# A two-level product whose next block's waits stand among the last terms of the current one

## The reference

```
gi = x_t @ W_ih + b_ih          # 64 x 1536
gh = h @ W_hh + b_hh            # 64 x 1536
r, z = sigmoid(i_r + h_r), sigmoid(i_z + h_z)
n = tanh(i_n + r * h_n)
h = (1 - z) * n + z * h
...
x + down( silu(gate(h)) * up(h) )   # operands quantised to fp8
```

## Time and profile before

| what | value |
|---|---|
| median of three runs | 2875.44 us (2875.31 to 2877.52) |
| profiled execution | its span is 2879.2 us; no other time is recorded for it |
| TensorE busy with matmuls | 2562.9 us, 89% of the span |
| DVE, ACT, POOL busy | 59%, 40%, 44% |
| matmuls at L1145 (whole) | 32768, mean 324 ns, 1026.0 us busy |
| matmuls at L1153 (low) | 16384, mean 324 ns, 756.5 us busy |
| mean granted clock of TensorE | 0.959 |

### The profile page before, as it was taken

The page is one execution under the profiler, slowest core; times in us unless marked ns, Lnnn a source line. Parts: engine busy times, 40 slices in busy tenths (PEclk is TensorE's granted clock), DMA queues, the critical chain, the costliest instruction groups (busy, mean ns, idle before and its releaser), DMA issues. The chain is left out here.

```text
span 2879.2 us, 154632 instructions
## 1 busy us (share of the span) xinstructions
PE 2562.9 (89%) x67605; PEld 1681.0 (58%) x67605; DVE 1685.2 (59%) x3398; ACT 1140.6 (40%) x2317; POOL 1262.3 (44%) x598
## 2 busy tenths in 40 slices
PE   2088999998889999999999999999996999999995
PEld 1066777776768888887675564655642444444442
DVE  8852222225632222225646778867592888888887
ACT  1321222225632222224702333323232777777773
POOL 0255666662046666664061363622700333333334
PEclk8599999999999999999999999999998999999998
DMA  6833222224422222226554253442432223232322
GB/s 193 239 85 77 74 73 71 73 71 112 131 63 71 74 73 70 73 71 167 152 135 127 92 151 118 115 156 85 129 143 93 74 84 95 84 95 84 95 63 53
DMA packets 234843, 293.74 MB, mean 102 GB/s; under 512 B 69581, under 2 KB 194023, under 8 KB 233895
## 3 DMA queue, kind: packets, MB, share of 16 engines
q1 hardware_dynamic: 212743, 240.84, 30.6%
q10 hardware_dynamic: 18304, 36.19, 3.6%
q0 software_dynamic: 3680, 15.21, 1.9%
HBM read 231.61 MB, written 60.45 MB: 101 GB/s over the span
## 5 line engine op out<-in xcount | busy, mean ns | idle before, releaser
L1145 PE MATMUL psum<-second_shared 64*32 64x384 f16 x32768 | 1026.0, 324 | 50.2 <-issue 31.3
L1153 PE MATMUL psum<-low_w,low_hot 64*32 64x384 f16 x16384 | 756.5, 324 | 2.0 <-issue 2.0
L1372 DVE TENSOR_SCALAR second_shared<-psum 32x384 f16<-32x384 f32 x496 | 272.3, 549 | 749.1 <-PE psum L1145 741.9
L953 POOL TENSOR_TENSOR low_hot<-first_shared,sum_mask 128x1024 f16<-128x1024 f16 x256 | 499.8, 1952 | 430.1 <-DVE first_shared L1359 183.8
L1145 PEld LDWEIGHTS psum<-second_shared 64*32 64x32 f16 x32768 | 561.5, 93 | 198.0 <-issue 89.8
L947 POOL TENSOR_TENSOR second_shared<-first_shared,whole_mask 128x2048 f16<-128x2048 f16 x128 | 462.5, 3614 | 460.1 <-PE psum L1145 348.2
L1044 ACT ACTIVATE second_shared<-psum 32x384 f16<-32x384 f32 x496 | 239.8, 483 | 801.9 <-PE psum L1145 795.9
L1233 PE MATMUL psum<-low_w,low_hot 64*64 64x384 f16 x12288 | 513.7, 326 | 19.9 <-issue 13.5
L1233 PEld LDWEIGHTS psum<-low_w,low_hot 64*64 64x64 f16 x12288 | 378.3, 108 | 150.4 <-issue 18.4
L310 PE MATMUL psum<-w_x,x_cols 128*64 128x512 f32 (+1 forms) x1856 | 312.0, 495 | 9.5 <-ACT x_cols L280 9.5
L1153 PEld LDWEIGHTS psum<-low_w,low_hot 64*32 64x32 f16 x16384 | 282.5, 93 | 56.8 <-issue 3.1
(11 more groups left out here) (286 smaller groups left out, 2746.6 us busy)
## 6 DMA issues: line engine op xcount, KB each, us to landing
low_w<-w_rows SPq DMA_DIRECT2D x384, 144.0 KB
low_w<-w_rows SPq DMA_DIRECT2D x256, 120.0 KB
second_shared<-w_rows SPq DMA_DIRECT2D x1024, 24.0 KB, 1.9
x_gates<-x_out ACTq DMA_DIRECT2D x58, 384.0 KB, 2.3
xg<-x_gates SPq DMA_DIRECT2D x58, 384.0 KB, 3.2
low_w<-w_rows SPq DMA_DIRECT2D x256, 72.0 KB
low_w<-w_rows SPq DMA_DIRECT2D x384, 48.0 KB
w_rows<-quantised SPq DMA_DIRECT2D x24, 384.0 KB, 4.9
```

Of the source, the lines that this page charges most:

```text
L953: nc.gpsimd.tensor_tensor(low_hot[:, buf].rearrange("p (s k) b -> p s k b", s=SUBS), low_a[:, slot, bass.ds(c, 1), :, :].rearrange("p a s ...
L1145: last = nc.tensor.matmul(run[m][u][j * Q:(j + 1) * Q, :], whole_hot[rows[u], m, sign, kk, j % 2 * Q:(j % 2 + 1) * Q], whole_w[rows[u], m, ...
L1153: nc.tensor.matmul(run[m][u][j * Q:(j + 1) * Q, :], low_hot[rows[u], m, kk, j % 2 * Q:(j % 2 + 1) * Q], low_w[rows[u], m, at:at + UC], sta ...
L1372: last = nc.vector.tensor_scalar(whole_w[u * B:u * B + Q, m, 0, bq, :], run[m][u][bq * Q:(bq + 1) * Q, :], 1.0 / HIGH_ONE, None, ALU.mult)
```

## The change

The block's waits become four functions, each with its own register work. They are called for the *next* block behind terms 11, 12, 13 and 14 (counted from 0) of the current one: low loads, whole loads, bases, hot rows. Before the loop they are made once for block (0, 0). The loop runs over c = 0 to 30; the turn c = 31 is written out behind it, its second block with no waits. For a turn with a constant c no register work is made. Each function waits for a constant first and then for the register's value, so there are eleven waits a block where nine were.

```
-                            with pe.Fori(0, NBK) as c:
+                            def bases_ready(c, m):
+                                based = c * 2 + (fine_no(t, m, 0) + 1)
+                                if not isinstance(c, int):
+                                    pe.compute_val(based)
+                                pe.wait_ge(base_v[0], fine_no(t, m, 0) + 1)
+                                for u in range(2):
+                                    pe.wait_ge(base_v[u], based)
+                                    pe.wait_ge(base_a[u], based)
+
+                            def weights_ready(c, m):
+                                w_ready = c * LOADED + (loaded_before(stage_of(t, m), m) + LOADED)
+                                if not isinstance(c, int):
+                                    pe.compute_val(w_ready)
+                                pe.wait_ge(w_in[m], loaded_before(stage_of(t, m), m) + LOADED)
+                                pe.wait_ge(w_in[m], w_ready)
...
+                            def terms(c, m, following):
+                                for kk in range(BK):
+                                    term(m, kk)
+                                    if following:
+                                        then = (c, 1) if m == 0 else (c + 1, 0)
+                                        if kk == BK - 5:
+                                            weights_ready(*then)
+                                        elif kk == BK - 4:
+                                            whole_ready(*then)
+                                        elif kk == BK - 3:
+                                            bases_ready(*then)
+                                        elif kk == BK - 2:
+                                            hots_ready(*then)
+
+                            weights_ready(0, 0)
+                            whole_ready(0, 0)
+                            bases_ready(0, 0)
+                            hots_ready(0, 0)
+                            with pe.Fori(0, NBK - 1) as c:
                                 for m in range(2):
-                                    based = c * 2 + (fine_no(t, m, 0) + 1)
...
-                                    for kk in range(BK):
-                                        term(m, kk)
+                                    terms(c, m, True)
+                            terms(NBK - 1, 0, True)
+                            terms(NBK - 1, 1, False)
```

More of the change, by code:

```diff
@@ L1165, in term @@
                                         last.then_inc(run_ok[u], 1)
-                            with pe.Fori(0, NBK) as c:
-                                for m in range(2):
-                                    based = c * 2 + (fine_no(t, m, 0) + 1)
[L1170 to L1181, removed]
-                                    for kk in range(BK):
-                                        term(m, kk)
@@ new lines, in weights_ready, with whole_ready @@
+                            def weights_ready(c, m):
[4 more added lines that the diff above has]
+                                pe.wait_ge(w_in[m], w_ready)
+                            def whole_ready(c, m):
+                                ready = c * WHOLE_LOADED + (t * NBK + 1) * WHOLE_LOADED
+                                if not isinstance(c, int):
+                                    pe.compute_val(ready)
+                                pe.wait_ge(whole_in[m], (t * NBK + 1) * WHOLE_LOADED)
+                                pe.wait_ge(whole_in[m], ready)
@@ new lines, in hots_ready @@
+                            def hots_ready(c, m):
+                                ready = c * 2 + (block_no(t, m, 0) + 2)
+                                if not isinstance(c, int):
+                                    pe.compute_val(ready)
+                                pe.wait_ge(hot_ok, block_no(t, m, 0) + 2)
+                                pe.wait_ge(hot_ok, ready)
+                            def terms(c, m, following):
[11 more added lines that the diff above has]
+                                            hots_ready(*then)
```

## The result

The changed kernel takes 2993.28 us, the median of four runs (2986.77 to 2998.96), against 2876.03 us: ratio 1.0407, 95% interval 1.0391 to 1.0422. That is +117 us where +99 was forecast; 2993 lies inside the range of 2960 to 2998. Here the profiled execution's own time is given too: 2998.96 us for a span of 2997.2, so 1.8 us lie around a span.

The account below looks back on a forecast made before the run. TensorE's time plus its holes was taken to bound the kernel. The terms 88 + 4.5 + 1.5 + 5 = +99 us, added to the 2875.44 us median, gave about 2975 us, range 2960 to 2998.

Parts of the forecast that it names:

- (b), the ring: Whole-load wait behind a block's 13th term closes a ring: period 8.96 us against 8.18, +0.78 a block, 88 us.
- (a), the hidden waits: Waits leave the border between blocks: gain 0.11 us inside a turn, 0.45 of 0.65 us at a return.
- (c), low loads, bases, hot rows: Their moved waits: low loads 0 to 0.1 us late, bases and hot rows there before the restart; nothing added.
- The bases' group: Five waits right behind the restart: 0 to 0.1 us a block, taken as 0, 11 us kept for the range.
- rival 3: The waits' own cost shows as well: +11 to +22 us, 2986 to 2997 us; chance 12%.
- (d), the written-out turns: Last turn of each product, new code to fetch: 0 to 4 us, taken as 2.5 each, +5 us.
- the first blocks: First product's first ten blocks: about 4.5 us, plus 1.5 us for a late load awaited three terms sooner.
- Rival 1: Loads are not late, so only the gain from hidden waits counts: 30 us faster, 2845 us; chance 4%.
- Rival 2: Granted clock falls to half for the three terms behind the hold: +165 us, 3140 us; chance 3%.
- Rival 4: Longer loop no longer stays on chip, each turn paying 3 us: +100 to +180, 3075 to 3155 us; chance 2%.

Follow-up runs that it names:

- fewer_loads_shifted: The changed kernel with a block's eight whole loads issued as four of twice the size, second product's loop shifted half a page: 2846.45 us, ratio 0.9889.
- last_turn_out: The kernel before, waits still at the head of each block, with only the last turn of each product written out: 2890.91 us, ratio 1.0043.
- late_whole: The changed kernel with the wait for the whole loads alone put back to the border, behind term 15: 3115.67 us, ratio 1.0825.
- changed_fewer_loads: The changed kernel with a block's eight whole loads issued as four of twice the size, loop not shifted: 3062.03 us, ratio 1.0606.
- by_arrival: The changed kernel with its waits ordered bases, hot rows, low loads, whole loads: 2950.01 us, spread 2910.37 to 3028.79, no ratio given.

## Why the prediction was right, point by point

- **(b), the ring.** Right in mechanism and nearly in size: 9.02 us a block where 8.96 was forecast, +0.85 where +0.78. 111 blocks (51 and 60) came to +94 us against 88 for 113. Three positions of the wait bear it out: four, three and one term behind it gave 9.51, 9.02 and 8.03 us, and loads in time gave 7.85.
- **(a), the hidden waits.** Under-sized, without consequence: I kept 0.2 us at a return, it became 0.02. Whatever a wait, the register work and the branch need is covered by the sequencer's lead once the awaited thing is there.
- **(c), low loads, bases, hot rows.** "Covered by (b) in any case" held for the sum. But the hold is a real one: between 887 and 1387 us the low loads are named for 15.1 us beside 25.0 for the whole ones, and without the whole loads' hold theirs makes 8.36 us a block. The bases' group (five waits here, six of the nine in the kernel before) costs nothing, and rival 3 (own cost) falls with the 7.85 us of fewer_loads_shifted.
- **(d), the written-out turns: the term that was mis-sized.** The forecast had 5 us, from the "issue" waits at L1145 alone in the first turn. Measured alone it is 14.1 us, and 15.7 in the changed kernel. Holes at L1153 belong to it too, so that a turn costs 5.7 us in the first product where I had 3 before hiding; in the second one hole alone is 3.1 us long (last_turn_out), and in the changed kernel the load for block 63 came 4.4 us later than before, with 3.4 us of waiting. 15.7 us lies outside the 0 to 8 that I had allowed this term. The total stayed inside the range because the 11 us kept for the bases' group were not needed; that is luck. This term is most of what was missing; the first blocks (+9.4 against 6) and the ring (+6) are the rest.
- **Rival 1** (faster) needed the landings before 6.0 us. fewer_loads_shifted made them so, and then it came true: 2846 us, where 2845 had been worked out. So close a match is partly luck: the written-out turns cost 12 us there where 5 were reckoned, and block 10, which had no place in that sum, gave some 8 back.
- **Rival 2** (the clock) did not happen in the changed kernel: the granted clock is 1.00 in both stretches with holes in every block. It did fall behind the slow branches of its neighbours. **Rival 4** (the loop no longer held) did not happen in the changed kernel, where the branches stay at 0.21 us, but it did in neighbours of it, at 14 to 15 us each.
- Of what was named as signs, more than a hundred waits for `second_shared` (113, 66.8 us in all), bursts about 9.0 us apart and the second product longer by 63 us all came. "About 1 us each" did not: a hold is split between low and whole loads.

## What to carry to other kernels

An early wait is free only if the awaited thing is already there at the new place: what is behind the waiting instruction is held up with it, and if that work sets off the next load, the wait closes a ring whose period is load + restart + the work left behind. So before waits are moved up, lay the landing times of each load beside the beat of the waiting engine, though no wait shows in the profile, and put the waits in the order of arrival; or shorten the chain of issues first. And time a loop of this length (some 1550 instructions) at two places in the program: in late_whole 200 us hung on a shift by 128 instructions.

## What the runs showed of the hardware that was not expected

- The branch at a loop's return takes 0.21 us, but 4.4 to 5.2 us in some executions of some returns, with nine instruction packets of 16 KB behind it, a stretch at half the granted clock and two slow blocks: 14 to 15 us in all. It went with a shift of 128 instructions (late_whole, changed_fewer_loads, by_arrival), and not with one of 256 (a single execution).
- Some 1550 instructions written out once cost 5.7 us in the first product and 8.8 in the second: a hole of 0.5 to 3.1 us in TensorE's work about every 256 instructions.
- TensorE's sequencer gets its lead back within a term: behind the restart at 314.68 register work and two semaphore instructions for the bases ran at 314.78 to 315.03, and the groups stayed 0.162 us apart.
- A whole load of twice the size takes 2.1 us to land instead of 1.8, and its issue no longer (0.83 us for two, where four of the smaller took 1.75).
